# Loading the filters of a group in two transfers in place of four

## The reference, cut to what matters

```python
x = x + _L0_conv_ref(_gn(x), L0_conv_h0, L0_conv_numerators, L0_conv_denumerator)
x = x + _L1_conv_ref(_gn(x), ...)      # patches of 8x8, queries, keys, values
x = x + _L2_conv_ref(_gn(x), L2_conv_filters, L2_conv_bias)
x = x + _L3_conv_ref(_gn(x), L3_conv_h0, L3_conv_numerators, L3_conv_denumerator)
```

```python
H = jnp.fft.rfft2(h_truncated, s=(2 * l1, 2 * l2))
H_full = h0 + H[0]
X = jnp.fft.rfft2(x, s=(2 * l1, 2 * l2), axes=(-3, -2))
Y = jnp.einsum('...hwi,ijhw->...hwj', X, H_full)
y = jnp.fft.irfft2(Y, s=(2 * l1, 2 * l2), axes=(-3, -2))
```

## Time and profile before

| | us |
|---|---|
| Three runs | 3484.6, 3485.92, 3451.22 |
| Their median | 3484.6 |
| The profiled execution, as timed | 3469.81 |
| Its span, first to last instruction | 3468.0 |
| PE busy in the span | 3237.8 (93%) |
| PE share of the chain that ended last, L795 and L809 | 9% and 2% (the chain as shown begins at 2961) |
| Group loop of the first layer | 680 to 1104 |
| Group loop of the last layer | 3014 to 3430 |
| DMA, mean over the span | 124 GB/s |

### The profile page before, as it was taken

The page is one execution under the profiler, slowest core; times in us unless marked ns, Lnnn a source line. Parts: engine busy times, 40 slices in busy tenths (PEclk is TensorE's granted clock), DMA queues, the critical chain, the costliest instruction groups (busy, mean ns, idle before and its releaser), DMA issues. The chain is left out here.

```text
span 3468.0 us, 82637 instructions
## 1 busy us (share of the span) xinstructions
PE 3237.8 (93%) x37272; PEld 2664.2 (77%) x37272; DVE 1565.3 (45%) x1926; ACT 1677.5 (48%) x1765; POOL 1250.9 (36%) x1018
## 2 busy tenths in 40 slices
PE   6999999889999699999899999999989997899998
PEld 6999998589999566666687776666668773489998
DVE  6787887411111433435765534333675444411112
ACT  3666665455652344444554534444454430455551
POOL 6888886155551102222530001222271000165550
PEclk9999999999999899999999999999999997999999
DMA  0333334877776312122133332221222345777776
GB/s 21 110 118 123 117 123 165 250 193 196 196 189 162 129 72 95 52 97 73 49 110 103 109 116 73 73 82 64 73 79 68 97 123 89 189 202 199 198 198 172
DMA packets 259577, 428.80 MB, mean 124 GB/s; under 512 B 28247, under 2 KB 106457, under 8 KB 257753
## 3 DMA queue, kind: packets, MB, share of 16 engines
q1 hardware_dynamic: 243242, 396.80, 39.5%
q10 hardware_dynamic: 15984, 26.72, 2.2%
HBM read 306.00 MB, written 113.77 MB: 121 GB/s over the span
## 5 line engine op out<-in xcount | busy, mean ns | idle before, releaser
L138 PE MATMUL m_bank<-xn,w 128*128 128x512 f32 x1536 | 617.9, 402 | 33.2 <-DVE m_store L1618 11.7
L139 PE MATMUL m_bank<-xn,w 128*128 128x512 f32 x1536 | 601.9, 392 | 0.0
L140 PE MATMUL m_bank<-xn,w 128*128 128x512 f32 x1536 | 601.5, 392 | 0.0
L795 PE MATMUL c_acc<-c_shifted,filt 128*32 128x192 f32 (+8 forms) x11264 | 457.6, 317 | 21.5 <-issue 21.5
L795 PEld LDWEIGHTS c_acc<-c_shifted,filt 128*32 128x32 f32 x11264 | 442.5, 158 | 32.5 <-issue 29.8
L605 ACT ACTIVATE filt<-filt 64x2048 f32<-64x2048 f32 (+3 forms) x256 | 419.3, 1735 | 13.6 <-DMA filt<-filters_dram 9.9
L592 POOL TENSOR_TENSOR filt<-filt 64x1408 f32<-64x1408 f32 x64 | 254.2, 3972 | 475.7 <-DMA filt<-filters_dram 475.7
L138 PEld LDWEIGHTS m_bank<-xn,w 128*128 128x128 f32 x1536 | 290.4, 189 | 174.4 <-issue 77.8
L129 ACT ACTIVATE w<-raw_weights 128x2048 fp32r<-128x2048 f32 x96 | 372.8, 3884 | 102.2 <-PE m_bank L140 101.3
L133 DVE TENSOR_TENSOR w<-raw_weights,w 128x2048 fp32r<-128x2048 f32 x86 | 332.6, 3868 | 159.3 <-ACT w L129 159.3
L140 PEld LDWEIGHTS m_bank<-xn,w 128*128 128x128 f32 x1536 | 290.5, 189 | 62.7
(11 more groups left out here) (194 smaller groups left out, 6739.5 us busy)
## 6 DMA issues: line engine op xcount, KB each, us to landing
c_shifted<-spectrum_dram SPq DMA_DIRECT2D x256, 270.0 KB, 3.9
filters_dram<-stage SPq DMA_DIRECT2D x124, 512.0 KB, 3.6
filt<-filters_dram SPq DMA_DIRECT2D x248, 256.0 KB, 4.8
raw_weights<-in_L_conv_Wq SPq DMA_DIRECT2D x16, 2048.0 KB, 8.7
raw_weights<-in_L_conv_Wk SPq DMA_DIRECT2D x16, 2048.0 KB, 8.6
raw_weights<-in_L_conv_Wv SPq DMA_DIRECT2D x16, 2048.0 KB, 8.6
m_qf<-in_L_conv_Wout SPq DMA_DIRECT2D x128, 256.0 KB, 3.8
spectrum_dram<-c_shifted SPq DMA_DIRECT2D x116, 136.0 KB, 2.5
```

Of the source, the lines that this page charges most:

```text
L138: pe.matmul(out, w[0], x[0], start=first, stop=False)
L139: pe.matmul(out, w[0], x[1], start=False, stop=False)
L140: return pe.matmul(out, w[1], x[0], start=False, stop=last)
L795: mm = nc.tensor.matmul(acc[k % 2][phase][32 * s:32 * s + 32, 0:B, LAGS * kb:HALF], filt[:, k, phase, :, :, 4 * kb + s].rearrange("p j c - ...
```

## The change

A group's filters come in two transfers of 512 KB. Each still has 128 runs, now of 4 KB. The count that completes a group's filters falls from 64 to 32. The places of issue change with it: in the first layer ACT issues four transfers, behind the copies `v` = 5 to 8; at the start of the last layer SP issues four; in the steady loop the six pieces go out at 0, 2 (filters) and 5, 6, 7, 8 (rows). At the start of the group loop the waits of the pieces of group 2 are 0, 1 (filters), 3, 5, 6, 7 (rows), with the filters of group 3 at 6 and 7, and its rows at 8 to 11 as before.

```diff
 def load_filters(eng, filt, scratch, layer, g, k, q):
-    return eng.dma_start(filt[0:64, k, EVEN:SUM, 4 * q:4 * q + 4].rearrange("p h j c n -> p h (j c n)"),
-                         scratch["filters"][g:g + 1, :, 4 * layer + q].rearrange("o (h p) j n -> p (o h) (j n)", h=2))
+    return eng.dma_start(filt[0:64, k, EVEN:SUM, 8 * q:8 * q + 8].rearrange("p h j c n -> p h (j c n)"),
+                         scratch["filters"][g, :, 4 * layer + 2 * q:4 * layer + 2 * q + 2].rearrange("(h p) m j n -> p h (m j n)", h=2))
...
-    SPREAD = (0, 1, 2, 3, 5, 6, 7, 8)
+    SPREAD = (0, 2, 5, 6, 7, 8)
...
-            if m < 4:
+            if m < 2:
                 load_filters(eng, filt, scratch, layer, g, k, m).then_inc(filt_in[k], 16)
             else:
-                load_rows(eng, g, k, m - 4)
+                load_rows(eng, g, k, m - 2)
...
-            for m in range(8):
+            for m in range(6):
                 if m:
-                    sp.wait_ge(progress, m)
+                    sp.wait_ge(progress, m + min(m - 1, 2))
                 piece(sp, 2, 2, m)
                 if m >= 4:
                     piece(sp, 3, 3, m - 4)
-            for m in range(4, 8):
-                sp.wait_ge(progress, 4 + m)
+            for m in range(2, 6):
+                sp.wait_ge(progress, 6 + m)
                 piece(sp, 3, 3, m)
...
-                pool.wait_ge(filt_in[k], 64 * (n + 1))
+                pool.wait_ge(filt_in[k], 32 * (n + 1))
...
-                if staged is not None and FETCH_AT <= v < FETCH_AT + 4 * EARLY:
+                if staged is not None and FETCH_AT <= v < FETCH_AT + 2 * EARLY:
...
-                    k, q = divmod(v - FETCH_AT, 4)
+                    k, q = divmod(v - FETCH_AT, 2)
```

More of the change, by code:

```diff
@@ L707, in _ @@
                 for k in range(EARLY):
-                    for q in range(4):
+                    for q in range(2):
                         load_filters(sp, filt, scratch, layer, k, k, q).then_inc(filt_in[k], 16)
@@ L909, in _ @@
                 op.then_inc(cols_ready, 1)
-            dve.wait_ge(filt_in[0], 64)
+            dve.wait_ge(filt_in[0], 32)
             dve.wait_ge(filt_summed, 1)
@@ L973, in _ @@
                     if v == min(TURN_AT):
-                        act.wait_ge(filt_in[0], 64)
+                        act.wait_ge(filt_in[0], 32)
                         act.wait_ge(filt_summed, 1)
@@ L980, in lower_half @@
                 n, k = divmod(g, RING)
-                act.wait_ge(filt_in[k], 64 * (n + 1))
+                act.wait_ge(filt_in[k], 32 * (n + 1))
                 for phases in (slice(EVEN, SUM), slice(SUM, 3)):
```

## The result

The changed kernel is slower by one per cent: 3500.6 us against 3465.5 us (medians of 20 runs each), ratio 1.0103, 95% interval 1.0082 to 1.0124. A second comparison (12 runs against 35) gave 1.0065, interval 1.0034 to 1.0096. So the loss is between 0.3 and 1.2%, 22 to 36 us by the two ratios. The profiled execution took 3526.3 us (span 3524.5), 56.5 us more than the span before. Not all of that is the change's.

What follows compares the result with a forecast made beforehand. PE was taken to bound the group loops, its gaps being late instruction fetches. Terms 11 - 3 + 0 - 1 = +7 us, set on 3477.2 us, gave 3484 us, range 3450 to 3522.

Steps and rivals of the forecast that it cites:

- SP's issues: Group loops: SP issues 120 transfers fewer but is no one's bottleneck there, so 0.
- Rival A: Group loops: instruction fetches slip in between runs, so transfer size is hidden; effect 0 - 1, time 3476 us; chance 0.25.
- rival B: Group loops: cheaper runs empty the DMA queues and more small gaps close; -15 us, 3462 us; chance 0.17.
- DMA time of a filter load: Filter loads: a 512 KB transfer takes an engine 2.2 us, between 1.97 and 2.42, giving back 0.45 us a group.
- Less DMA load: Group loops: 4% less load shortens the queue a fetch meets, small gaps shrink by a tenth; -3 us, ends 0 and -10.
- How long one transfer holds an engine: Steady loop: fetches wait 34 us more behind longer transfers, a third reaching PE; 11 us, ends 0 and 40.
- 134 of 173 are in time: Group loops: 39 of 173 instruction fetches come too late, 23%, and the other 134 are in time.
- Start of the loops: First groups of both loops: the 17.9 us of large gaps stay; 0, with +5 or -5 us in one loop.
- ACT in the row stage: First layer's row stage: four ACT issues go, largely hidden in waits for stores; -1 us, ends -2.5 and +4.
- Rival C: Both loops: every fetch meeting a filter transfer pays the extra 0.6 us in full; 40 us slower, 3516 us; chance 0.13.
- Issue waits of 50 to 55 us: Sign in the changed profile: PE's waits without a semaphore in the two loops, 43.8 us before, become about 50 to 55.

Runs made afterwards that it cites:

- halves_steady_only: Kernel before with two 512 KB filter transfers at progress 0 and 2 in the steady loop alone (groups 4 to 31); loops 856 us, ratio 1.0060.
- halves_start_only: Changed kernel with 512 KB transfers for the first four groups of each layer only, the steady loop in four of 256 KB; loops 841 us, ratio 1.0031.
- small_in_pairs: Kernel before with its four 256 KB transfers in the steady loop issued in pairs, at progress 0, 0, 2, 2; loops 836 us, ratio 0.9997.

## Why the prediction was right and wrong

Right: what bounds the loops, that PE's gaps are missing instructions, that they grow when a transfer grows with the number of its runs kept, and that the waits of POOL and ACT for filters and SP's issues are hidden. Rival A is refuted by the doubled size's +29 us, rival B by rows of the loops themselves.

Wrong: the size, +7 us where the loops alone lost 29 and the whole 22 to 36. The step that failed is how much of the fetches' longer waiting reaches PE. By the prediction's steps:

- *DMA time of a filter load.* The 0.246 us of the `Wout` loads is not the price of a filter run. Measured with full engines: 0.274 us a packet, 2.47 us a transfer, the upper end of 2.42. In the middle of the loops it is 8 x 0.27 = 2.16 us, near the 2.2 that was taken, but there the old runs were cheaper too, 1.12 in place of 1.21 us. The Trainium skill's rule on the ports ("SBUF — State Buffer", "Door 1: The DMA port swizzle"), which the prediction set beside it, agrees to within 4%: in the loops 4 KB took 0.27 us in one run and 0.28 in two, so run length bought next to no bandwidth into partitions 0 to 63.
- *Less DMA load*, -3 us, fell with it. The engines work 9 us a group in both kernels.
- *How long one transfer holds an engine*, the mis-sized term: 11 us, measured 21 (halves_steady_only). By the prediction's rule the additional waiting is 34 us, or 67 x 0.63 = 42 with the price of full engines; it was not measured by itself. The prediction let a third of it reach PE; 21 us is a half to three fifths. The third rested on "134 of 173 are in time". This count said how many fetches were late, not by how little the others were in time: over half of the blocks were entered at most 1.8 us after their packet ended, as at a gap, so that for them nearly all further waiting reaches PE. The rule itself, that a fetch waits for the whole transfer, doesn't cover the kernels with longer runs, so the 34 us is no more than an estimate.
- *Start of the loops*, 0: measured 7 us (halves_start_only), a little above the scatter. *ACT in the row stage*, -1: measured +2 to +5, near the end of +4 that was given.
- Rival C, 40 us, came nearer to the time than the forecast did, but not by its own sign, 80 us or more of issue waits. "Issue waits of 50 to 55 us" became 60 to 64; for the loops' time even that is too little, since the waits undercount.

The Trainium skill's rule in "DMA: Bandwidth & Descriptors", "Queues, rings and completion order", that an engine drains a whole packet of descriptors before it turns to another queue, agrees with small_in_pairs against halves_steady_only: two transfers in a row cost the loops 20 us less than one of double size at the same moment, as if a fetch got in between the two. It doesn't explain why 64 runs of the same bytes lose 17 to 35 us less than 128 (35 with 32 partitions in place of 64); what within a transfer lets a fetch through stays open. The same page, in "Rules for kernel authors", asks for 1 MiB and more in a transfer for bandwidth: here this was the slowest version of all, 2.7% above before. Bandwidth was not what was short, with the engines busy for 0.72 and 0.73 of the steady time.

## What to carry to other kernels

Where an engine's program is written out and long, its instructions are one more stream on the DMA engines, and here it was a late one. Look for "issue" gaps without a semaphore, count whether they lie whole blocks of instructions apart, and see whether each ends shortly after a packet of the instruction queue; then ask how early the other packets are, not only how many are late. If they are late, try large background loads in smaller transfers with few, long runs for each engine and fewer partitions, even if SP issues more. In this kernel that gave 0.6%. A load that nobody waits for can still cost time: take it away once, and see what the loops do without it.

## What the hardware showed unasked

A single instruction on DVE, L133, one of 86 alike, took 25 us in 6 of 17 profiles and under 5 us in all others, in kernels of every kind. Of the two profiles of the kernel before (ns min/median/max):

```profile
L133 DVE TENSOR_TENSOR w<-raw_weights,w x86: 3792/3818/4565, 1194.9 to 2659.3; 128x2048 fp32r<-128x2048 f32 x86
```

```profile
L133 DVE TENSOR_TENSOR w<-raw_weights,w x86: 3789/3814/25248, 1192.8 to 2678.6; 128x2048 fp32r<-128x2048 f32 x86
```

PE waits 18 to 20 us for it. That is why these two profiled executions of one kernel differ by 19 us (3468.0 and 3487.0). It would also explain that the 20 runs of before in the first comparison fall into one group at 3451 to 3466 us and another at 3479 to 3495, but those have no trace. What stops the instruction wasn't looked into.
